# Attention passes of a graph network over steps in place of quanta, with scanned maxima

## The reference

```python
# layer 0: mean of neighbours, then a linear map
neigh_sum = segment_sum(x[col], row);  out = (neigh_sum / (deg + 1e-6)) @ W.T + b
# layer 1: an edge MLP, mean over edges
eh = relu(concat([feat[src], feat[dst]]) @ W_edge.T)
# layer 2: two GAT convolutions, 16 heads of 8; self loops are appended to the edges
e = leaky_relu(al_s[src] + al_d[dst], 0.2)
m = segment_max(e, dst);  ex = exp(e - m[dst]);  denom = segment_sum(ex, dst)
out = segment_sum(xh[src] * (ex / (denom[dst] + 1e-16))[:, :, None], dst)
# layer 3: dot product attention, 2 heads of 64, no added self loops
alpha = (q[dst] * k[src]).sum(-1) / 8;  a = exp(alpha - segment_max(alpha, dst)[dst])
agg = segment_sum(a[:, :, None] * v[src], dst) / max(segment_sum(a, dst), 1e-16)
```

## Time and profile before

| | us |
|---|---|
| runs | 5859.1, 5897.09, 5904.79; median 5897.09 |
| profiled execution | 5831.78 |
| its span | 5830.1 |
| POOL busy in the span | 3866.3 (66%) |
| TensorE matmuls busy | 3718.0 (64%) |
| VectorE busy | 3393.5 (58%) |
| ScalarE busy | 1507.5 (26%) |

### The profile page before, as it was taken

One profiled execution on the slowest core, in us unless ns is written; L12 is line 12 of the kernel. 1 busy time (PEld: TensorE's weight loads), 2 busy tenths in 40 slices (PEclk: granted clock), 3 DMA queues, 4 the chain that ended last, 5 costly groups with the idle time before them and its releaser, 6 DMA issues. The chain is left out here.

```text
span 5830.1 us, 119852 instructions
## 1 busy us (share of the span) xinstructions
PE 3718.0 (64%) x37479; PEld 3280.9 (56%) x37480; DVE 3393.5 (58%) x9662; ACT 1507.5 (26%) x4156; POOL 3866.3 (66%) x3926
## 2 busy tenths in 40 slices
PE   1344444457777775577776756677766567777785
PEld 0233333346666664566666645666666457777774
DVE  3322222343333335677777776777777878888886
ACT  0000000132222222333333332333332233333331
POOL 1677777427777770677777727777777157777773
PEclk9755555566666665676667656766676676666666
DMA  4211111111111110222222342222224333333335
GB/s 103 57 49 49 49 49 49 33 34 51 50 49 50 49 50 16 65 65 65 65 65 65 63 41 65 65 65 65 65 65 62 34 92 103 103 103 103 104 104 69
DMA packets 227643, 370.81 MB, mean 64 GB/s; under 512 B 73550, under 2 KB 150606, under 8 KB 227535
## 3 DMA queue, kind: packets, MB, share of 16 engines
q0 software_dynamic: 138176, 323.74, 23.9%
q1 hardware_dynamic: 89378, 46.01, 2.7%
HBM read 342.26 MB, written 27.89 MB: 63 GB/s over the span
## 5 line engine op out<-in xcount | busy, mean ns | idle before, releaser
L1047 POOL DMA_INDIRECT GT<-table,srcI x3880 | 3838.6, 989 | 1819.0 <-issue 1324.1
L1298 PE MATMUL psA<-V,O 128*128 128x144 f32 (+1 forms) x4944 | 1166.1, 425 | 0.5 <-DVE V L1406 0.5
L1298 PEld LDWEIGHTS psA<-V,O 128*128 128x128 f32 x4944 | 1109.8, 321 | 6.9 <-DVE V L1406 0.8
L1069 PE MATMUL psA<-zerob 1*128 1x258 bf16 (+1 forms) x704 | 179.8, 406 | 667.7 <-issue 647.9
L1060 DVE TENSOR_TENSOR O<-iotab,slotT 128x1024 f32<-128x1024 bf16 x88 | 108.5, 1234 | 723.8 <-PE psA L1116 722.6
L1060 DVE TENSOR_TENSOR Ob<-iotab,slotT 128x1024 bf16<-128x1024 bf16 x397 | 483.8, 1219 | 4.9 <-DMA table<-GT 4.1
L1069 PEld LDWEIGHTS psA<-zerob 1*128 1x128 bf16 x704 | 72.9, 125 | 731.5 <-issue 707.7
L1290 PE MATMUL psS<-newM,Ot 128*128 128x16 bf16 (+1 forms) x7416 | 243.3, 170 | 365.7 <-DVE newM L1393 365.7
L1290 PEld LDWEIGHTS psS<-newM,Ot 128*128 128x128 bf16 x7416 | 216.0, 101 | 431.7 <-DVE newM L1393 431.7
L1237 ACT ACTIVATE resc<-diff 128x32 f32<-128x32 f32 (+1 forms) x309 | 67.7, 219 | 1489.1 <-DVE acc L1424 1452.2
L1259 PE MATMUL psD<-quantD,Ot 128*128 128x16 bf16 (+1 forms) x7416 | 435.3, 217 | 5.8 <-ACT quantF L1222 5.6
(11 more groups left out here) (227 smaller groups left out, 5994.0 us busy)
## 6 DMA issues: line engine op xcount, KB each, us to landing
GT<-table,srcI POOLq DMA_INDIRECT x3880
first<-first_dram SPq DMA_DIRECT2D x206, 64.0 KB
first_dram<-GT SPq DMA_DIRECT2D x18, 448.0 KB, 6.2
table<-GT SPq DMA_DIRECT2D x40, 144.0 KB, 1.9
table<-GT SPq DMA_DIRECT2D x20, 256.0 KB, 2.1
table<-O SPq DMA_DIRECT2D x20, 128.0 KB, 1.8
table<-GT SPq DMA_DIRECT2D x20, 128.0 KB, 1.8
out<-X SPq DMA_DIRECT2D x1, 2496.0 KB
```

The costliest lines, as they stand in the source:

```text
L1047: eng.indirect_dma_start(out=GT[:, p.k, j, 0:table.shape[1]], out_offset=None, in_=table, in_offset=bass.IndirectOffsetOnAxis(ap=srcI[:, p ...
L1069: eng.matmul(psA[:, a:a + 2, 0:w], zerob[0:1, 0:P], zerob[0:1, 0:2 * w], start=True, stop=False, skip_group_check=True)
L1298: ins = eng.matmul(psA[:, p.q * QS + j // Q, 0:VW], O[:, p.q, j, :], V[:, p.q, j, 0:VW], start=j % Q == 0, stop=j % Q == Q - 1)
```

## The change

The softmax passes drop the quanta and go over the same 704 steps as the other passes: 88 groups each. The second set of index tables, `stage`, and `Q` go. What that needs:

- TensorE's edge matmuls read `nodeD` or `nodeQ` at register addresses, 24 for a group, after a load of 8 registers.
- The sums go into 9 places in `psA` (three in each of three banks), at register addresses, after three zeroing matmuls of 510 columns. There is one set of places, and its zeroing waits for `added` of the group before.
- VectorE keeps a maximum for each step. A carry from the last group (`carried`) and two scans over a group's 8 steps, one forward and one backward, give each step its block's maximum so far; resets of -1e30 part the blocks. One scaling of the first block in `acc` and one add of all 9 places take the place of two and two.
- GAT: ScalarE notes each step's maximum in `nodeM` (`act_note`). The self loops are no longer seeded in `acc`: the pass leaves the sums without them, and the stretch after it merges them (`self_shares_1`, `self_shares_exp`, `self_shares_2`, `self_and_sums`).
- ScalarE copies the flags and resets (`act_flags`), and rescale waits for `scaled` of the group two before, which VectorE issues in the same turn.

```diff
-    QS = G // Q
-    NGQ = -(-((STEPS + NB * (Q - 1)) // Q) // QS)
+    PLACES, STRIDE = 9, 170
...
             def pe_toedge(eng, p):
-                eng.wait_ge(*staged(p.g))
+                b = loaded(eng, "blocks", blk, p.g, G, NB - 1)
                 eng.wait_ge(*onehotT(p.g))
                 eng.wait_ge(*prodded(p.g - 1))
                 for j in range(G):
+                    to = dst_logits[:, j, :] if gat else psD[:, j, :]
                     for part in range(3):
-                        ins = eng.matmul(psD[:, j, 0:dw], Ot[:, p.k, j, :], quantD[:, p.q, j // Q, part, 0:dw],
+                        ins = eng.matmul(to, Ot[:, p.k, j, :], at_part(nodeD if gat else nodeQ, b[j], part),
                                          start=part == 0, stop=part == 2)
...
             def pe_sums(eng, p):
+                off = loaded(eng, "places", blk_off, p.g, G, STRIDE * 7 + 4)
+                eng.wait_ge(*added(p.g - 1))
+                apart(eng)
+                for n in range(3):
+                    eng.matmul(flatA[:, 512 * n:512 * n + 3 * STRIDE], zerob[0:1, 0:P], zerob[0:1, 0:3 * STRIDE],
+                               start=True, stop=False, skip_group_check=True)
                 eng.wait_ge(*values(p.g))
                 eng.wait_ge(*onehot32(p.g))
-                eng.wait_ge(*qadded(p.g - 2))
+                apart(eng)
                 for j in range(G):
-                    ins = eng.matmul(psA[:, p.q * QS + j // Q, 0:VW], O[:, p.q, j, :], V[:, p.q, j, 0:VW],
-                                     start=j % Q == 0, stop=j % Q == Q - 1)
+                    ins = eng.matmul(flatA[:, bass.ds(off[j], VW)], O[:, p.q, j, :], V[:, p.q, j, 0:VW], start=False,
+                                     stop=j == G - 1, skip_group_check=True)
...
+            def act_note(eng, p):
+                b = loaded(eng, "blocks", blk, p.g, G, NB - 1)
+                eng.wait_ge(*newMed(p.g))
...
+                    eng.copy(at_block(nodeM, b[j], h), by_step(newM[:, p.q, 0:HG])[:, :, j]).then_inc(noted.sem, 1)
...
             def act_rescale(eng, p):
                 eng.wait_ge(*drop(p.g))
-                eng.wait_ge(*qadded(p.g - 2))
+                eng.wait_ge(*scaled(p.g - 2))
...
             def dve_max(eng, p):
-                after(eng, p, 0)
-                for u in range(1, QS):
-                    before(eng, p, u)
-                    after(eng, p, u)
...
+                eng.scalar_tensor_tensor(out=by_step(t)[:, :, 0], in0=was, scalar=flag, in1=by_step(t)[:, :, 0], op0=ALU.add,
+                                         op1=ALU.max).then_inc(carried.sem, 1)
...
+                eng.tensor_tensor_scan(run, reset[:, p.q, 0, 0:HG], t, -BIG, ALU.add, ALU.max).then_inc(forward.sem, 1)
...
+                eng.tensor_tensor_scan(now[:, ::-1], reset[:, p.q, 1, 0:HG][:, ::-1], run[:, ::-1], -BIG, ALU.add, ALU.max)\
+                   .then_inc(newMed.sem, 1)
...
+            def dve_add(eng, p, b):
+                a = acc[:, bass.ds(b, PLACES), 0:VW].rearrange("p (n k) w -> p n k w", n=3)
                 eng.wait_ge(*sums(p.g))
-                eng.wait_ge(*qscaled(p.g, u))
-                eng.tensor_tensor(a, a, psA[:, p.q * QS + u, 0:VW], ALU.add).then_inc(qadded.sem, 1)
+                eng.wait_ge(*scaled(p.g))
+                eng.tensor_tensor(a, a, psP, ALU.add).then_inc(added.sem, 1)
...
+        def self_and_sums(eng, n):
+            c = D // HEADS1
+            of = n.at(acc)[:, :, 0:DH].rearrange("p g (h c) -> p g h c", h=HEADS1)
+            eng.tensor_tensor(heads(n.Y, HEADS1), of[:, :, :, 0:c], wide(n.at(nodeM), c), ALU.mult).then_inc(own.sem, 1)
+            eng.tensor_tensor(heads(n.Y2, HEADS1), heads(n.at(selfX), HEADS1), wide(n.at(nodeS), c), ALU.mult)\
+               .then_inc(denom.sem, 1)
```

More of the change, by code:

```diff
@@ L14 @@
 G = 8
-Q = 4
 RING = 4
@@ L183, in program, with loaded @@
         reg_sets = {}
-        def loaded(eng, which, table, g, n, most):
+        def loaded(eng, which, table, g, n, most, of=None):
             if (eng.engine, which) not in reg_sets:
@@ L385, in _ @@
-                marks["src of steps"] = count
-                do(eng.tensor_tensor, dst_f, dst_f, wide(sidx[:, 3, 0:SC], P), ALU.subtract)
-                marks["slots of steps"] = count
-                eng.wait_ge(spread, BLOCKS)
-                do(eng.tensor_scalar, brow[:, 0, :], vall[0][:, 0:NB], float(Q), None, ALU.mult)
-                do(eng.tensor_copy, brow[:, 1, :], vall[0][:, NB:2 * NB])
-                marks["block rows out"] = count
-                eng.wait_ge(tables_turned, SRC0)
@@ L453, in _ @@
-                do(eng.tensor_copy, row[0][:, 0:NQ], blkq[:, :])
+                marks["first"] = count
+                eng.wait_ge(tables_turned, SRC)
+                do(eng.tensor_copy, srcT[:, :], psN[:, 0:SC, :].rearrange("p c s -> p (c s)"))
+                marks["src out"] = count
+                eng.wait_ge(block_loaded, 16)
+                blk_g, rel_g = (t[:, :].rearrange("p (g j) -> p g j", j=G) for t in (blk, blk_rel))
+                do(eng.tensor_tensor, rel_g, blk_g, blk_g[:, :, 0:1].to_broadcast([1, SP_ // G, G]), ALU.subtract)
@@ L491, in _ @@
             def _(eng):
[L492 to L499 removed]
+                eng.wait_ge(prepared, marks["steps"])
@@ L501, in _, with spread_row @@
+                for c in range(SC):
+                    for n, of in enumerate((e_rows, s_rows)):
+                        eng.indirect_dma_start(
+                            out=rows[n][:, c, :].bitcast(I32), out_offset=None, in_=of,
+                            in_offset=bass.IndirectOffsetOnAxis(ap=tb_i[:, 0, c:c + 1], axis=0),
+                        ).then_inc(fetched, 16)
             @block.tensor
             def _(eng):
-                def spread_row(to, of, n):
+                def spread_row(of, n):
@@ L521, in _ @@
-                eng.matmul(vall[0][:, NB:2 * NB], bcol[:, 2:3].to_broadcast([P, P]), ident[:, 0:NB],
-                           start=True, stop=True).then_inc(spread, 1)
-                eng.wait_ge(prepared, marks["src of steps"])
-                turn(rows[3], SC)
-                eng.wait_ge(prepared, marks["src out"])
-                turn(rows[2], SC)
-                eng.wait_ge(prepared, marks["slots out"])
+                spread_row(row[0], T)
                 for k, slot in enumerate((W0, WEA, WEB, WN, W1R, W2R)):
```

531 lines of the change are left out of this document (236 added, 295 removed).

## The result

The changed kernel takes 6521.38 us (6516.82 to 6524.99) against 5893.99 before: **1.1078, 95% interval 1.1038 to 1.1119**. The sign was forecast; the time was not: 401 us above the forecast of 6120 and outside the range to 6350. The profiled execution took 6516.82 us, its span is 6515.1, against 5830.1.

A forecast was written before the change was run, and what follows sets the result against it. The VectorE-TensorE loop was to replace POOL's gathers as bound: GAT +94, dot +151, preparation -38, self loops +18, in all +225 on 5832 us, 6057; with 65 to the median, 6120 us, range 5950 to 6280 (wider 5870 to 6350).

The forecast's parts named there:

- What bounds the kernel: Softmax passes: POOL's gathers bound, 10.05 us a GAT group; VectorE-TensorE loop 0.7 us under it, in dot sharing the bound.
- Step 1: GAT: zeroing of the single-buffered sums waits for VectorE's 1296-element add; TensorE starts at 5.25 us instead of 3.98.
- Step 2: TensorE zeroing ahead of the sums: three matmuls of 510 columns, 1.28 us with 0.1 behind, sums at 6.63 us.
- Step 3: Edge matmuls at register addresses: up to 3.1 us a group if serial; costed at nothing in GAT, exposed in dot.
- serial case: Register load and issue of GAT's edge matmuls fully uncovered: +3.1 us a group, 6665 us; chance 0.04.
- rival C: TensorE's sequencer isn't far enough ahead to hide GAT's load and register instructions; chances 0.10 (first case) and 0.04 (serial).
- first case: GAT's load issued with only 2.2 us of sums still to run: +1.3 us a group, 6350 us; chance 0.10.
- the 6210 us: By the skill's 64-entry TensorE queue, the load would wait for about half of the sums: some 6210 us.
- Dot: Dot pass: edge matmuls have no array work ahead, so loads and issue are exposed; 13.7 us a group, +151 us.
- Off the loops: Outside the loops: act_note's ScalarE copies wait-free, gathers hidden, preparation -38 us, self loops and related work +18 together.
- rival B: TensorE gets 2.4 GHz through zeros and sums: GAT 11.0, dot 11.5 us a group, 5700 us; chance 0.08.
- D: Path as forecast but shorter because carried-over waits vanish: GAT 11.6, dot 12.6 us a group, 5900 us; chance 0.08.

The follow-up runs named there:

- the fixed-address kernel: Changed kernel with GAT's and dot's edge matmuls at fixed addresses, no register load or register instruction per matmul; 0.973 of before, GAT 12.12 us a group.
- the load kept: Changed kernel with edge matmuls at fixed addresses, register load kept in the source, values unused; 0.998 of before on the slow chip, 0.972 repeated elsewhere.

## Why the prediction was wrong

**What bounds the kernel** was right. The loop through VectorE and TensorE took POOL's place; its releases are what POOL waits for.

**Step 1**, the zeros wait for the add: shown by the early add. Forecast 5.25 us behind the logit sum, measured 5.40. Sound, though moving it was worth 1.64 us and not 0.7: the zeros came 1.1 us earlier, since the segment scan moved with the add, and the sums were 0.6 us shorter at the risen clock.

**Step 2**, the zeroing: 1.36 us from the first zero to the first sum, forecast 1.38. Leaving it out is worth 1.1.

**Step 3 failed in GAT.** I wrote that TensorE's sequencer "is through with the new sums at 6.5" and has "5.0 us of array work (sums and maxima, to 11.6) as cover for a load and 3.1 us of issue". That takes the lead for unlimited. Measured: load 0.7 and register instructions 2.56 of 3.24 us a group, 570 us for 176 groups, and 15.36 for 12.3. This is the serial case of rival C, which I put at 6665 us with a chance of 0.04; its first case, with a lead of 2.2 us, had 6350. The two GAT loops exceed their forecast by some 450 us and not by 570, because other things went the other way: 12.12 us a group instead of 12.3 with this cost away (32 us), 15.21 in the mean of a whole pass instead of 15.36 (26), and before 10.31 over its whole passes, not 10.05 (53).

The error behind it was in reading. A load is issued at 1720.3 with 2.2 us of sums still to run, and I carried over the 2.2 us. But in that pass eight transposes stand between the sums and the load:

```profile
1722.26 1.06 PE L1174 MATMUL psT<-identb,Ob 128*128 128x128 bf16 x8
```

What the trace shows is eight pairs of the sums and eight transposes still to begin, 16 pairs. Behind 24 maxima matmuls at 0.035 us, 16 pairs are 0.56 us. With the count in place of the time, rival C's serial case would have been the forecast: 12.3 + 3.1 = 15.4.

The Trainium skill, Advanced Engine Details and Errata, Engine Queue Depths, has 64 entries for TensorE. The lead that the runs show, 10 to 16 pairs or 20 to 32 instructions, is a third to a half of that, and the 6210 us that I took from the rule was too low as well.

**Dot** came out at 13.6 us a group over the whole pass and 13.9 in the window of the table, against 13.7, from its pieces. Its edges have no array work ahead, so all was exposed and I had counted all. The early loads confirm 1.3 us for them.

**Off the loops.** `act_note`, eight copies of 0.22 us, costs the loop nothing by the waits: in GAT from 2700 to 3200 TensorE and VectorE wait for each other and for issue alone. No run leaves it out. Preparation gained 42 us for 38. GAT's two stretches grew by 591 us; 544 of them lie between the logit sums of the first and the last group of a pass (1054 and 1049 us before, 1323 and 1323 after), the other 47 are self loops and the passes' ends, for which I had 18.

**The clock** (rival B): sums in GAT ran at the low level, 4.08 to 4.21 us from 2700 to 3200, as taken. I didn't foresee that it would rise where issue time was removed: dot's sums went from 3.4 to 3.8 us down to 2.05 in most turns, and the fixed-address kernel, which should have come to 5915 beside 5894 by its terms, ran at 0.973 of before. Why it rises there in dot and hardly in GAT (sums 4.06 us in the mean) stays open. D's direction, shorter loops, was nowhere in the changed kernel.

**The base.** I added 65 us between the profiled execution and the median. After the change that distance is 5 us, so 60 of them were not there, and the terms missed by 460 us and not by 401: GAT 479 too low, dot 21 too high, and 2 from the rest. That the miss reads 401 and not 460 is luck.

## What to carry to other kernels

How far TensorE's sequencer runs ahead was a number of instructions here, not a time. Convert it with the duration of the instructions that stand just ahead of the place in question, and read it in the trace as what is still to run before the load, every kind of it. Issue-bound work (register loads, matmuls at register addresses) belongs directly behind few long matmuls, not behind many short ones; here that order alone was 2.65 us of a 15.4 us group.

When a loop is already near two bounds, put single-buffered work (zeroing, the add that frees it) where its engine waits anyway. Steps and scans in place of quanta lost 11% as written, and gained 6% once four pieces were reordered; the kernel before was not reordered in turn, so how much of the 6% steps and scans alone are worth stays open.

## What the runs showed of the hardware

- In the changed kernel a register instruction and its matmul go out every 0.13 us (24 from 3212.2 to 3215.1), a load of eight registers takes 0.59. In the kernel whose loaded registers nothing used, the trace has no load at all.
- A gather of POOL that starts while VectorE runs an operation with both inputs in SBUF (values, one-hot) ends 0.8 us after that operation unless it would end later anyway, 1.72 and 1.93 us instead of 0.95. Beside the product of dot, which reads PSUM, none of the changed kernel (18 gathers, 5300 to 5600) was longer than 0.95. The Trainium skill, GPSIMD Engine Reference, Key points, says that GpSimd shares its SBUF interfaces with VectorE and contends with instructions of two SBUF inputs; the trace agrees, with these times.
- TensorE's two clock levels make the same 16 sum matmuls 2.05 or 3.83 us long. The kernel that interleaves f32 sums with bf16 edges has a mean granted clock of 0.52 over 206 us of GAT, the one with the edges first 0.63. What decides the level stays open.
- On one chip of several, before takes 7813 to 7821 us, a third more, and the changed kernel 1.049 of it; VectorE there waits more than 3000 us for events outside the engines. Slower kernels were slower there too and faster ones faster (but for the load kept, 0.998, which can't be told from 1); the sizes were others, and so was the order of two of them.
